# Attention scores of two heads side by side in the row halves of TensorE, and the shared expert's two projections in one matmul group

## The chip, the cores and the metric

The kernel runs on 1 core of one Trainium2 chip. The metric is the time of one execution on the device in microseconds (us). A core has TensorE (PE, with its weight loads shown apart as PEld), VectorE (DVE), ScalarE (ACT), GpSimd (POOL) and the DMA queues, most of them issued from SyncE (SP). Each engine works through its own list of instructions in order, and they wait for each other by semaphores.

## What is computed

One transformer layer on x of 8 sequences of 256 tokens with 128 channels, all in float32. Attention has 16 heads of 8 channels; the feed-forward part has a shared expert and 16 routed ones (top 2), each of width 64.

```
xn = layernorm(x)
qkv = xn @ Wqkv + bqkv ; q, k = rope(q), rope(k)
probs = softmax(q @ k.T / sqrt(8))            # 8 x 16 heads, 256 x 256 each
attn = (probs @ v) @ Wout + bout
router = sigmoid(xn @ gate_w + gate_b) ; top 2 values, divided by their sum
mlp(x, wg, wu, wd) = (silu(x @ wg) * (x @ wu)) @ wd
ffn = xn + mlp(xn, shared) + sum over the top 2 of value * mlp(xn, expert)
out = x + attn + ffn
```

## The kernel before

**Tiles.** Two sequences make a group of 512 tokens, 4 groups in all. The feed-forward part is cut into chunks of 128 hidden rows, 9 to a group and 36 in all, numbered n: chunk 0 of a group (n = 0, 9, 18, 27) is the shared expert and fills only 64 rows, and the other eight hold two experts each. The attention is cut into 32 steps q of four heads. Two steps make a half (h = 0 to 15), that is eight heads of one sequence.

**Blocks.** One list of 40 blocks, blk = -6 to 33, sets the order on every engine. Block blk holds chunk n = blk + 6, the row maxima of the scores of step q = blk + 4, the exponentials of the scores of step blk, and the product with the values of step blk - 1. Each block has four places, i = 0 to 3, one head at each. The tables `LATE_A` and `EARLY_B` say in which block the rarer work stands (transposes of x, projections of q, k and v, the router, the transposes and projection of the attention's output).

**Scores.** q and k are split into bfloat16 parts, laid out so that six products of parts stand as 48 rows (`KROWS`). A pair of heads shares a slot: head r of the pair has rows 48r to 48r + 47 of `q_hat`, and `k_hat` holds each head's rows with zeros in the other head's rows, so that a matmul over 96 rows gives one head. `max_scores` (L508) makes two 256-column matmuls for a head into one of the two PSUM banks `S1a`, `S1b`, whose maxima DVE takes (`TENSOR_REDUCE`, L1000). For each half POOL splits the negated maxima into three bfloat16 parts (`negate_maxima`, L1072 to L1076, result `md`), PE transposes them (L497, `maxima_to_rows`) into an S1 bank, DVE copies them to `mT` (L872), and a DMA puts them as 6 more rows below the 96 of `q_hat` (L336). `exp_scores` (L529) then computes scores minus maximum over 102 rows into `S2a` or `S2b`, and ACT takes the exponential (L734) into `probs`. `attend` (L548) multiplies four heads' probabilities with the values, four matmuls of 32 columns side by side. PE takes one bank at a time: scores for a bank wait only until that bank's former contents are read.

**Feed-forward.** `up(n, "hg")` makes the gate product of chunk n in three matmuls (float32 as high and low parts, L386 to L388) into bank `FA`, and `up(n, "hu")` the up product into `FB`. ACT takes the tanh of FA (L746) and from n = 6 on copies FA to `gate` (L750). DVE multiplies tanh + 1 with FB (`gu`, L988; for n < 6 two operations, L1009 and L985). POOL weights gate and product (L1112, L1114, L1101), and `down` (L581) of chunk n - 2 adds to bank `Y`.

**Order on PE in a block.** i = 0: exponential's scores, maximum's scores, gate product, in every second block the transposes of the maxima of a half; i = 1: `attend`, scores; i = 2: `EARLY_B` work, scores; i = 3: `down`, `LATE_A` work, scores, up product. "Scores" are two matmuls into an S2 bank and two into an S1 bank. POOL and DVE take their parts of the block in the same order; POOL does `negate_maxima` first, then the weighting, then residuals and the splits of the next group's q and k.

## Time and profile before

| | us |
|---|---|
| median of 3 runs | 243.12 |
| lowest, highest | 242.80, 243.15 |
| the profiled execution | 242.69 |
| its span, first to last instruction | 240.0 |
| PE, DVE, POOL, ACT busy | 216.0, 168.7, 161.2, 137.1 |

A row of the timeline gives the start of the first instruction in it, the time until the last one's end, engine, line, operation, output <- inputs, shapes and count, and in brackets the idle time before it with the instruction that ended it. On PE the pair such as 96*128 is the rows and columns of the array that the matmul uses. Matmuls are pipelined: a row's duration contains the way through the array, so what a matmul costs its follower is the distance of the starts. A row can merge several instructions.

### The profile page before, as it was taken

Reading aid. Unit: us, or ns where it says so; the run is one execution under the profiler, and the core shown is the slowest. Engines: PE = TensorE matmul, PEld = TensorE weight load, DVE = VectorE, ACT = ScalarE, POOL = GpSimd, SP = SyncE. Lnnn points to the kernel's source line nnn. Section 1 sums busy time; section 2 is a strip of 40 time slices with the busy share of each in tenths; the row PEclk is TensorE's granted clock in tenths of the full one; section 3 lists DMA queues with packets and bytes.
Section 4 is the critical chain, followed back from the end, with each engine's and each line's share of the span. In section 5 each row is a group of like instructions: output and inputs, shape, how many; then the busy total and the mean of one; then the engine's idle time right before and its main releaser. Section 6 shows DMA issues by size and latency. Waiting matters only on the chain.

```text
span 240.0 us, 4717 instructions
## 1 busy us (share of the span) xinstructions
PE 216.0 (90%) x1576; PEld 134.1 (56%) x1576; DVE 168.7 (70%) x374; ACT 137.1 (57%) x257; POOL 161.2 (67%) x236
## 2 busy tenths in 40 slices
PE   0485698898989999989999999999999999999993
PEld 0354454464655666666756656666756656675552
DVE  5997869999585766998656768976666666655221
ACT  2455111155568665656566665667575866667662
POOL 9186763789847259888848295999893855637802
PEclk9997789999999999999999999999999999999999
DMA  6925354620527240502662414116516450211101
GB/s 231 358 66 152 104 163 131 189 92 2 182 71 219 80 145 5 153 0 75 204 202 60 159 46 126 30 54 175 150 31 190 142 155 17 76 50 43 47 0 44
DMA packets 35952, 26.51 MB, mean 110 GB/s; under 512 B 4236, under 2 KB 30156, under 8 KB 35916
## 3 DMA queue, kind: packets, MB, share of 16 engines
q1 hardware_dynamic: 35292, 25.33, 34.9%
q10 hardware_dynamic: 636, 0.88, 1.0%
q8 instruction: 12, 0.20, 0.3%
q14 instruction: 12, 0.10, 0.1%
HBM read 18.53 MB, written 7.47 MB: 108 GB/s over the span
## 4 chain that ended last, share of the span: by engine, by line
PE 74%; DVE 11%; DMA 5%; SPq 4%; issue 2%; ACT 2%; POOL 1%; DVEq 0%; ACTq 0%; POOLq 0%
PE PV L548 12%; PE Y L581 12%; PE S2b L529 7%; PE S2a L529 6%; PE S1a L508 5%; PE S1b L508 5%; PE FB L386 3%; PE FB L387 3%; PE FB L388 3%; PE FA L387 3%; PE FA L386 3%; PE FA L388 3%; DMA x_sb<-in_x 2%; DVE mx L1000 2%; PE FA L441 2%
## 5 line engine op out<-in xcount | busy, mean ns | idle before, releaser
L1000 DVE TENSOR_REDUCE mx<-S1a 128x2 f32<-128x512 f32 x65 | 44.6, 686 | 17.3 <-PE S1a L508 17.3
L1000 DVE TENSOR_REDUCE mx<-S1b 128x2 f32<-128x512 f32 x63 | 43.2, 685 | 19.2 <-PE S1b L508 19.0
L734 ACT ACTIVATE probs<-S2b 128x512 f32<-128x512 f32 x62 | 37.1, 598 | 29.5 <-PE S2b L529 29.5
L734 ACT ACTIVATE probs<-S2a 128x512 f32<-128x512 f32 x62 | 37.1, 599 | 17.2 <-PE S2a L529 14.6
L1114 POOL TENSOR_TENSOR gu<-gu,gate 128x512 f32<-128x512 f32 (+1 forms) x30 | 38.2, 1274 | 9.1 <-DVE gu L988 7.6
L581 PE MATMUL Y<-gu,wd_sb 128*128 128x512 f32 (+1 forms) x72 | 37.3, 599 | 0.3 <-POOL gu L1101 0.3
L746 ACT ACTIVATE th<-FA 128x512 f32<-128x512 f32 (+1 forms) x36 | 21.5, 597 | 25.3 <-PE FA L388 25.1
L548 PE MATMUL PV<-probs,vx 128*32 128x256 f32 x512 | 35.1, 384 | 0.2 <-ACT probs L734 0.2
L1112 POOL TENSOR_TENSOR gate<-gate,wbc 128x512 f32<-128x512 f32 x27 | 34.5, 1279 | 0.7 <-DMA wbc<-route_w 0.6
L508 PE MATMUL S1a<-k_hat,q_hat 96*128 96x256 bf16 x130 | 25.2, 275 | 1.5 <-DVE mx L1000 1.5
L508 PE MATMUL S1b<-k_hat,q_hat 96*128 96x256 bf16 x126 | 24.3, 274 | 1.6 <-DVE mx L1000 1.4
L529 PE MATMUL S2a<-q_hat,k_hat 102*128 102x256 bf16 x124 | 24.1, 276 | 0.0
L529 PE MATMUL S2b<-q_hat,k_hat 102*128 102x256 bf16 x124 | 24.1, 275 | 0.0
L988 DVE SCALAR_TENSOR_TENSOR gu<-th,FB 128x512 f32<-128x512 f32 (+1 forms) x30 | 20.4, 679 | 1.8 <-PE FB L388 1.6
L548 PEld LDWEIGHTS PV<-probs,vx 128*32 128x32 f32 x512 | 16.0, 109 | 9.7 <-ACT probs L734 4.7
L529 PEld LDWEIGHTS S2b<-q_hat,k_hat 102*128 102x128 bf16 x124 | 9.2, 97 | 20.8 <-issue 17.2
L386 PE MATMUL FB<-xT_hi,wu_hi 128*128 128x512 f32 (+1 forms) x36 | 17.7, 492 | 3.0 <-ACT sig L685 2.7
L386 PE MATMUL FA<-xT_hi,wg_hi 128*128 128x512 f32 (+1 forms) x36 | 17.5, 486 | 0.6 <-ACT xT L667 0.4
L750 ACT ACTIVATE gate<-FA 128x512 f32<-128x512 f32 (+1 forms) x30 | 17.7, 590 | 0.0
L1072 POOL TENSOR_SCALAR md<-mx 128x16 bf16<-128x16 f32 x16 | 3.3, 205 | 21.3 <-DVE mx L1000 21.3
L508 PEld LDWEIGHTS S1b<-k_hat,q_hat 96*128 96x128 bf16 x126 | 11.7, 99 | 7.1 <-DVE mx L1000 4.9
L529 PEld LDWEIGHTS S2a<-q_hat,k_hat 102*128 102x128 bf16 x124 | 9.1, 98 | 11.2 <-issue 6.3
(163 smaller groups left out, 408.4 us busy)
## 6 DMA issues: line engine op xcount, KB each, us to landing
wbc<-route_w SPq DMA_DIRECT2D x64, 128.0 KB, 3.0
q_hat<-q_parts SPq DMA_DIRECT2D x32, 96.0 KB, 2.6
k_hat<-k_parts SPq DMA_DIRECT2D x32, 96.0 KB, 2.6
k_parts<-parts SPq DMA_DIRECT2D x8, 192.0 KB, 2.1
q_parts<-parts SPq DMA_DIRECT2D x8, 192.0 KB, 2.2
x_sb<-in_x SPq DMA_DIRECT2D x4, 256.0 KB, 3.9
q_parts<-parts SPq DMA_DIRECT2D x8, 128.0 KB, 2.1
k_parts<-parts SPq DMA_DIRECT2D x8, 128.0 KB, 2.1
```

Of the source, the lines that this page charges most:

```text
L386: nc.tensor.matmul(bank, w_hi, m_hi, start=start, stop=False)
L508: last = nc.tensor.matmul(bank[:, t * T:(t + 1) * T], q_hat[0:MROW, slot, pair, t * P:(t + 1) * P], k_hat[0:MROW, slot, pair, r, :], start ...
L529: last = nc.tensor.matmul(exp_bank(head)[:, s * T:(s + 1) * T], k_hat[0:KALL, slot, pair, r, s * P:(s + 1) * P], q_hat[0:KALL, slot, pair, ...
L548: last = nc.tensor.matmul(PV[32 * j:32 * j + 32, hg * T:(hg + 1) * T], vx[:, (b // GB) % 2, SB * (b % GB) + s, r, NQ * hg + j, :], probs[: ...
L581: nc.tensor.matmul(Y[:], wd_sb[0:rows, c, :], gu[0:rows, n % GU_SLOTS, :], start=c == 0, stop=c == NCH - 1).then_inc(down_done, 1)
L734: nc.scalar.activation(probs[:, head % (2 * NQ), :], exp_bank(head)[:], ACT.Exp, scale=SCALE).then_inc(exp_done, 1)
L746: nc.scalar.activation(th[0:rows, n % 2, :], FA[0:rows, :], ACT.Tanh, scale=0.5).then_inc(th_ready, 1)
L750: nc.scalar.activation(gate[0:rows, n % 2, :], FA[0:rows, :], ACT.Copy, scale=0.5 if n % NCH == 0 else 1.0).then_inc(fa_read, 1)
L988: nc.vector.scalar_tensor_tensor(gu[0:rows, m % GU_SLOTS, :], th[0:rows, m % 2, :], 1.0, FB[0:rows, :], ALU.add, ALU.mult).then_inc(fb_rea ...
L1000: nc.vector.tensor_reduce(mx[:, (q // QB) % 2, (q // 2) % 2, :, q % 2, i], S1[use % 2][:].rearrange("p (t s) -> p t s", t=SB), axis=AX.X, ...
L1112: after(nc.gpsimd.tensor_tensor(gates, gates, wbc[:, g % 2, c - 1, :], ALU.mult))
L1114: nc.gpsimd.tensor_tensor(product, product, gates, ALU.mult).then_inc(gu_weighted, 1)
```

## The change

The scores move into row halves of the array. Head r of a pair now has its 48 rows at partition 64r of `q_hat` and `k_hat`, and its three maxima rows behind them, so that a matmul runs over 48 (51 with the maxima) rows in one half of the array. `max_pair` and `exp_pair` take two heads at a time, in opposite halves and into both banks in turn. `k_hat` loses its zeros (two memsets and the wait for them go), and the ones and the maxima come by two DMAs each where one stood. Which head of a pair is at which half alternates with the step (`score_row_half`).

The order in a block changes: the gate product stands first; scores come in two lots, at i = 0 and i = 2; transposes of the maxima, `down` and `LATE_A` work move to i = 2 ahead of the second lot, so the transposes of a half come half a block earlier. On ACT the tanh comes at i = 0 and the copy of the gate after the second exponential.

For the shared expert the gate and up weights stand side by side, one group of three matmuls fills FA (gate in rows 0 to 63, up in rows 64 to 127), and no second group is made; DVE multiplies straight from FA at i = 1, and POOL weights that product as any other. For n = 0 one DVE operation less is made.

```diff
-    last = nc.tensor.matmul(bank[:, t * T:(t + 1) * T], q_hat[0:MROW, slot, pair, t * P:(t + 1) * P],
-                            k_hat[0:MROW, slot, pair, r, :], start=True, stop=True)
-last.then_inc(s1_ready, 1)
...
+banks = [take_s(("max", q * NQ + i)) for i in (first, first + 1)]
+for t in range(SB):
+    for i, bank in zip((first, first + 1), banks):
+        pair, rows = NQ * hg + i, HROWS * score_row_half(q, i)
+        last = nc.tensor.matmul(bank[:, t * T:(t + 1) * T],
+                                q_hat[rows:rows + KROWS, slot, pair, t * P:(t + 1) * P],
+                                k_hat[rows:rows + KROWS, slot, pair, :], start=True, stop=True)
+        if t == SB - 1:
+            last.then_inc(s1_ready, 1)
...
 if head < NQ * FOUR_BANKS + 2:
     if head >= 2:
-        pe.wait_ge(exp_done, head - 1)
+        pe.wait_ge(exp_done, head)
...
+for s in range(SB):
+    for i in (first, first + 1):
+        pair, rows = NQ * hg + i, HROWS * score_row_half(q, i)
+        last = nc.tensor.matmul(exp_bank(q * NQ + i)[:, s * T:(s + 1) * T],
+                                k_hat[rows:rows + KALL, slot, pair, s * P:(s + 1) * P],
+                                q_hat[rows:rows + KALL, slot, pair, :], start=True, stop=True)
...
 for i in range(NQ):
+    if i == 0 and n < NCHUNKS:
+        up(n, "hg")
     if i == 1 and 0 <= blk - 1 < NBLK:
         attend(blk - 1)
     if i == 2:
         for kind, g in early_b(blk):
             fill_b(kind, g)
-    if i == 3 and 0 <= n - 2 < NCHUNKS:
-        down(n - 2)
-    if i == 3:
+        if 0 <= n - 2 < NCHUNKS:
+            down(n - 2)
+        if negated_half(blk) is not None:
+            maxima_to_rows(negated_half(blk))
         for kind, g in late_a(blk):
             fill_a(kind, g)
-    if 0 <= blk < FOUR_BANKS:
-        exp_scores(blk, i)
-    if 0 <= q < NBLK:
-        max_scores(q, i)
-    if i == 0 and n < NCHUNKS:
-        up(n, "hg")
+    if i % 2 == 0 and 0 <= blk < FOUR_BANKS:
+        exp_pair(blk, i)
+    if i % 2 == 0 and 0 <= q < NBLK:
+        max_pair(q, i)
...
-    if i == 0 and transposed_half(blk) is not None:
-        maxima_to_rows(transposed_half(blk))
-    if i == 3 and n < NCHUNKS:
+    if i == 3 and n < NCHUNKS and n % NCH:
         up(n, "hu")
...
+    if m % NCH == 0:
+        dve.wait_ge(th_ready, m + 1)
+        dve.wait_ge(shared_gate, m // NCH + 1)
+        nc.vector.scalar_tensor_tensor(product, tanh, 1.0, FA[I:2 * I, :], ALU.add, ALU.mult).then_inc(fa_read, 1)
+        return
```

How this moves PE's instructions is seen in block 18, from `attend` (PV) to its third lot of scores. Before:

```order
L548 MATMUL PV<-probs,vx 32x256 x8
L529 MATMUL S2b<-q_hat,k_hat 128x256 x2
L508 MATMUL S1b<-k_hat,q_hat 128x256 x2
L482 MATMUL FB<-ident_sb,attn 128x128 x2
L529 MATMUL S2a<-q_hat,k_hat 128x256 x2
L508 MATMUL S1a<-k_hat,q_hat 128x256 x2
L581 MATMUL Y<-gu,wd_sb 128x512
L529 MATMUL S2b<-q_hat,k_hat 128x256 x2
L508 MATMUL S1b<-k_hat,q_hat 128x256 x2
```

After (L575 is `attend`, L611 `down`, L517 the transposes of the maxima, L555 the exponential's scores, L530 the maximum's):

```order
L575 MATMUL PV<-probs,vx 32x256 x8
L502 MATMUL FB<-ident_sb,attn 128x128 x2
L611 MATMUL Y<-gu,wd_sb 128x512
L517 MATMUL S1a<-identb_sb,md 24x128 x2
L555 MATMUL S2a<-q_hat,k_hat 128x256
L555 MATMUL S2b<-q_hat,k_hat 128x256
L555 MATMUL S2a<-q_hat,k_hat 128x256
L555 MATMUL S2b<-q_hat,k_hat 128x256
L530 MATMUL S1b<-k_hat,q_hat 128x256
L530 MATMUL S1a<-k_hat,q_hat 128x256
L530 MATMUL S1b<-k_hat,q_hat 128x256
L530 MATMUL S1a<-k_hat,q_hat 128x256
```

Four lots of two and two score matmuls, each lot for one head, have become lots of eight for two heads, banks in turn. `down` and the transposes of the maxima stand before the second lot.

The boundary from there to the next block's `attend`, before:

```order
L529 MATMUL S2a<-q_hat,k_hat 128x256 x2
L508 MATMUL S1a<-k_hat,q_hat 128x256 x2
L386 MATMUL FA<-xT_hi,wg_hi 128x512
L387 MATMUL FA<-xT_hi,wg_lo 128x512
L388 MATMUL FA<-xT_lo,wg_hi 128x512
L497 MATMUL S1b<-identb_sb,md 24x128 x2
L548 MATMUL PV<-probs,vx 32x256 x8
```

After, from the gate product on:

```order
L406 MATMUL FA<-xT_hi,wg_hi 128x512
L407 MATMUL FA<-xT_hi,wg_lo 128x512
L408 MATMUL FA<-xT_lo,wg_hi 128x512
L555 MATMUL S2a<-q_hat,k_hat 128x256
L555 MATMUL S2b<-q_hat,k_hat 128x256
L555 MATMUL S2a<-q_hat,k_hat 128x256
L555 MATMUL S2b<-q_hat,k_hat 128x256
L530 MATMUL S1b<-k_hat,q_hat 128x256
L530 MATMUL S1a<-k_hat,q_hat 128x256
L530 MATMUL S1b<-k_hat,q_hat 128x256
L530 MATMUL S1a<-k_hat,q_hat 128x256
L575 MATMUL PV<-probs,vx 32x256 x8
```

The gate product stands ahead of all scores of the block, and the transposes of the maxima are gone from the place before `attend`.

On ACT, a block with the attention's transpose read at i = 1, before:

```order
L746 ACTIVATE th<-FA 128x512
L750 ACTIVATE gate<-FA 128x512
L734 ACTIVATE probs<-S2b 128x512
L697 ACTIVATE attnT<-FB,bias_sb 128x256
L734 ACTIVATE probs<-S2a 128x512
L734 ACTIVATE probs<-S2b 128x512
L734 ACTIVATE probs<-S2a 128x512
```

After (L772 tanh, L763 exponential, L782 copy of the gate, L726 the transpose's read):

```order
L772 ACTIVATE th<-FA 128x512
L763 ACTIVATE probs<-S2a 128x512
L763 ACTIVATE probs<-S2b 128x512
L782 ACTIVATE gate<-FA 128x512
L726 ACTIVATE attnT<-FB,bias_sb 128x256
L763 ACTIVATE probs<-S2a 128x512
L763 ACTIVATE probs<-S2b 128x512
```

The copy of the gate (L750, now L782) has moved from right behind the tanh to behind the first two exponentials of the block.

## Rows read from the trace of the kernel before

**Rows 1.** The page: busy time of each engine and TensorE's granted clock in 40 slices.

```profile
PE 216.0 (90%) x1576; PEld 134.1 (56%) x1576; DVE 168.7 (70%) x374; ACT 137.1 (57%) x257; POOL 161.2 (67%) x236
...
PEclk9997789999999999999999999999999999999999
```

**Rows 2.** Busy time by stretch: us, PE, PEld, DVE, ACT, POOL, clock, DMA share, GB/s.

```profile
28.00:62.00 34.00, 30.35 (x165) 17.50 (x165) 29.50 (x64) 11.19 (x22) 23.91 (x40) 0.95 0.39 117
62.00:222.00 160.00, 158.02 (x1239) 99.46 (x1237) 112.38 (x218) 104.59 (x196) 111.74 (x170) 1.00 0.35 103
222.00:240.00 18.00, 13.99 (x122) 7.89 (x121) 4.13 (x12) 9.56 (x19) 6.42 (x6) 1.00 0.08 30
...
98.50:105.30 6.80, 6.80 (x56) 4.51 (x56) 6.60 (x21) 4.52 (x9) 6.30 (x11) 1.00 0.27 70
```

**Rows 3.** Waits of PE from 62 to 222 us: total, times, longest.

```profile
PE S1a L508 <- DVE mx L1000: 0.8, 1, 0.8
PE S1b L508 <- DVE mx L1000: 0.6, 1, 0.6
PE FA L386 <- ACT xT L667: 0.4, 1, 0.4
PE PV L548 <- ACT probs L734: 0.2, 1, 0.2
```

**Rows 4.** Timeline of PE over one block, from 178.6 us.

```profile
178.60 0.39 PE L388 MATMUL FA<-xT_lo,wg_hi 128*64 128x512 f32 x1
178.92 0.23 PE L497 MATMUL S1a<-identb_sb,md 128*24 128x128 bf16 x1
...
179.04 1.03 PE L548 MATMUL PV<-probs,vx 128*32 128x256 f32 x13
180.00 0.39 PE L529 MATMUL S2b<-q_hat,k_hat 102*128 102x256 bf16 x2
180.23 0.38 PE L508 MATMUL S1b<-k_hat,q_hat 96*128 96x256 bf16 x2
180.45 0.38 PE L529 MATMUL S2a<-q_hat,k_hat 102*128 102x256 bf16 x2
180.67 0.38 PE L508 MATMUL S1a<-k_hat,q_hat 96*128 96x256 bf16 x2
180.89 1.02 PE L581 MATMUL Y<-gu,wd_sb 128*128 128x512 f32 x2
181.75 0.60 PE L433 MATMUL FA<-ident_sb,pv_sb 128*128 128x128 f32 x4
182.19 0.38 PE L529 MATMUL S2b<-q_hat,k_hat 102*128 102x256 bf16 x2
182.41 0.38 PE L508 MATMUL S1b<-k_hat,q_hat 96*128 96x256 bf16 x2
...
183.33 0.39 PE L529 MATMUL S2a<-q_hat,k_hat 102*128 102x256 bf16 x2
```

**Rows 5.** Timeline of PE around the shared expert's `down`, 64 rows of the array.

```profile
82.87 0.38 PE L508 MATMUL S1a<-k_hat,q_hat 96*128 96x256 bf16 x2
83.18 1.12 PE L581 MATMUL Y<-gu,wd_sb 64*128 64x512 f32 x2
84.24 0.66 PE L433 MATMUL FA<-ident_sb,pv_sb 128*128 128x128 f32 x4
```

**Rows 6.** Timeline at the first transposes of maxima: PE's `down`, POOL's last part, transposes, copy.

```profile
43.04 1.02 PE L581 MATMUL Y<-gu,wd_sb 128*128 128x512 f32 x2
...
45.42 0.20 POOL L1076 TENSOR_SCALAR md<-mrest 128x16 bf16<-128x16 f32 x1
...
45.95 0.28 PE L497 MATMUL S1b<-identb_sb,md 128*24 128x128 bf16 x2
...
46.34 0.27 DVE L872 COPY mT<-S1b 24x256 bf16<-24x256 bf16 x1
```

**Rows 7.** Timeline at the first router weights, 26.5 to 27.7 us.

```profile
26.56 0.38 DVE L865 TENSOR_TENSOR wtok<-wsel 128x64 f32<-128x64 f32 x1
26.87 0.67 DVE L985 TENSOR_TENSOR gu<-FB,th 64x512 f32<-64x512 f32 x1
...
27.69 0.27 PE L470 MATMUL FB<-ident_sb,wtok 128*64 128x128 f32 x1 [1.55 <-DVE gu L985]
```

**Rows 8.** The page's groups: busy time, mean ns, idle before.

```profile
L1000 DVE TENSOR_REDUCE mx<-S1a 128x2 f32<-128x512 f32 x65 | 44.6, 686 | 17.3 <-PE S1a L508 17.3
...
L734 ACT ACTIVATE probs<-S2b 128x512 f32<-128x512 f32 x62 | 37.1, 598 | 29.5 <-PE S2b L529 29.5
```

224 lines of the change are left out of this document (117 added, 107 removed).

## The prediction

> **What bounds the kernel now.** I read the page first: PE is busy for 216.0 of 240.0 us, DVE for 168.7, and TensorE's clock is at nine tenths or more from the seventh of the 40 slices on [rows 1]. The table by stretch splits the run: from 62 to 222 us PE is busy for 158.02 of 160 us and no other engine for more than 112.38; from 28 to 62 us DVE is the fullest, with 29.50 of 34; the last 18 us are a tail with little in it [rows 2]. In the long middle PE's waits add up to 2.0 us [rows 3]. So there every bit of stream taken from PE counts, as long as its partners keep up. Then comes PE's timeline over one block [rows 4], read by the distances of starts, since the durations (0.38 us) contain the way through the array. Two score matmuls take 180.00 to 180.23, and eight take 180.00 to 180.89: 0.111 us each. `down` takes 180.89 to 181.75, 0.86. A three-matmul group takes 0.70 (182.41 + 0.22 to 183.33). `attend` with the transposes of the maxima takes 178.92 to 180.00. The block is a full stream: 16 score matmuls are 1.78 us of a plain block, with two such groups (1.40), `down` (0.86) and `attend` (1.07) 5.1.
>
> **Row halves.** Each lot of eight becomes four rounds of two matmuls side by side, if the halves run together. A round should cost what one matmul costs, 0.111 us. The trace has no matmuls in two row halves at once; it has four in column strips, where 13 of the 16 of `attend`, of 256 columns, end 1.03 us after the first start [rows 4], where one after another they would take more than 13 x 0.111 = 1.44. The bounds for a round are 0.111 (both together) and 0.222 (one after another). I take 0.111, because the column strips are the nearest case. That is 0.89 us less for each of the 27 blocks (1 to 27) with both kinds of scores: **-24.0 us**. At 0.222 it is 0.
>
> The Trainium skill, "TensorE: Matmul & The Clock Gate", section "Measured speedup vs the span model", gives 3.07 times for four row tiles, not 4. By that a round would cost 1.3 times a matmul, and 7 us of the 24 would be gone; rows of this case can't decide it, since none has two row tiles at work.
>
> **What the halves cost.** The shared expert's `down` already works in 64 rows, and shows the price of changing the division of the array [rows 5]. The scores before it start at 82.87, and two take 0.22, so it could start at 83.09; it starts at 83.18: 0.09 for the change. From there to the next instruction is 1.06 us against 0.86 for the same work in 128 rows [rows 4], 0.20 more: 0.09 for the change back, and 0.11 because the first weights of a float32 operand no longer load under the matmul before. The step into the 24-column transposes costs the same 0.09 (178.60 + 0.23 to 178.92) [rows 4].
>
> A block before has two changes (into `attend` and out). After, it has five: gate product to scores, scores to `attend`, `attend` to `down`, `down` to scores, scores to up product. Three more at 0.09 are 0.27. The first weights lie bare twice more, before `down` and before the up product: 0.21. Together 0.48 a block, 27 blocks: **+13.0 us**. The low bound is 0.27 a block, 7.3 us, if the weights still load in time. The scores' own weights are bfloat16, and behind `attend` today two matmuls start 0.23 apart as elsewhere [rows 4], so I count nothing for them.
>
> **Transposes of the maxima** (every second block, 14 times in this stretch). They lie between `down` and scores, where they cost one change more: 0.09 x 14 = 1.3. And they hold an S1 bank. From their start to the end of DVE's copy is 45.95 to 46.61 [rows 6], 0.66 us; `max_pair` takes both banks before it starts, and PE has only the transposes, a change and four exponential's scores to issue, about 0.43. The 0.23 left is a wait in the 7 of these blocks where no `LATE_A` work stands between and maxima follow: 1.6. Together **+2.9 us**.
>
> **Shared expert.** Three of the four (n = 9, 18, 27) are in this stretch. Each saves a group of three, 0.70, and its `down` follows `attend` and precedes scores in the same halves, so that the 0.29 of rows 5 and one change of 0.09 go: 1.08 x 3 = **-3.2 us**. DVE, ACT and POOL have as many operations for it as before (for n = 0 DVE has one of 0.67 less [rows 7]).
>
> **The partners.** A lot of exponential's scores now waits until both former banks are read. From lot to lot across the block's end: ACT can start 0.39 after the first start, and two exponentials of 0.598 [rows 8] end at 1.6; PE's own way is two half lots (0.44), 0.20 of change and weights, 0.70 + 0.70 for up and gate product, 0.09, together 2.13. Two maxima of 0.686 [rows 8] end 1.98 after the exponential's lot began (0.22 + 0.39 + 1.37), and are wanted at 2.35. The other distance, with `attend` and `down` in it, is 2.6. So the pairs are covered in a plain block, by 0.4 to 0.5 us; without that cover each would show in full. ACT has six operations of about 0.6 in a plain block and DVE 3.4 us (four maxima and a product), and the tanh that now comes before the first exponential falls into ACT's gap. Where it isn't covered is the block from 98.5: DVE is busy for 6.60 of 6.80 and POOL for 6.30 [rows 2]; it and its twin eight blocks later gain nothing and lose what they were counted: **+0.8 us**. POOL runs late in a few blocks, and the transposes of the maxima now ask for its result half a block earlier: **+1.0 us**, an estimate between 0 and 3.
>
> **The first 62 us.** DVE sets the pace there, and it lives on two banks in turn. With pairs it stands for about 0.4 us after its second read, unless other work fills that. Ten lots are in question; I count three (bounds 0 and 10 x 0.4): +1.2. The first transposes of maxima are wanted right after `down`, at 43.04 + 0.86 = 43.9; POOL's last part is ready at 45.62 [rows 6]. PE stands for up to 1.7 us there with `max_pair` queued behind, DVE behind that; I take 1.5. Against it, the router's transpose at 27.69 waited for a DVE read of FB (26.87 to 27.54) that is gone, while its input was ready at 26.94 [rows 7]: -0.6 on a chain that goes on by DMAs; and one DVE operation of 0.67 less. In sum **+1.5 us**.
>
> **At nothing.** Both memsets of `k_hat` ran while x was on its way. SP issues two more DMAs for the ones, before it has to wait for q and k. The maxima go by two DMAs of half the size; they start half a block earlier and are wanted in the second block after; if that lead were gone, each would cost its issue of some 0.4 us. The tail has changes that eat the halved scores.
>
> **Sum.** -24.0 + 13.0 + 2.9 - 3.2 + 0.8 + 1.0 + 1.5 = -8.0 us. The profiled execution took 242.69, of which 240.0 is the span and the rest stays, so 234.7; the median of the runs is 0.4 above it. I predict **235.1 us**, likeliest case 229 to 239.5.
>
> **Rivals.**
> (a) Slower: *the row halves run one after another*. The changes and bare weights stay, the 24.0 go: 259. The gain is nil where a round of two costs 0.147 us (27 x 8 rounds x (0.222 - 0.147) = 16). Against it: the column strips. Chance 0.07.
> (b) *Halves overlap in part*, since one weight path feeds both: a round between 0.13 and 0.17 gives 239 to 248, centre 243. Chance 0.13 (0.04 still faster, 0.02 the same, 0.07 slower).
> (c) *The pairs wait*: PE ahead, and the reads of both banks end last. At 0.2 us a block the gain shrinks by 5 to 240 or 241. For it: DVE has only 0.37 (2.35 - 1.98) of cover, and every operation beyond the plain ones eats from it. Chance 0.15 (0.02 of it the same). The Trainium skill, "TensorEngine Tiling (Array Packing)", section "PSUM Bottleneck", says that tiling speeds the engine up but not the reading of its results; by that, reading is next in line, which is this case.
> (d) *The first third loses more*: all ten lots stand (4.0), and POOL's lateness recurs at each transposes of maxima (0.5 x 14): 244 to 247. Chance 0.07.
> (e) Weights load in time after a change, and the waits are small: 13.0 - 7.3 = 5.7 less and a little more, 227 to 229. Chance 0.06.
>
> **Numbers.** The likeliest case has 0.52. Faster by over 0.2%: 0.52 + 0.06 + 0.13 + 0.04 = 0.75; within 0.2%, which is about what a measurement here can tell apart: 0.04; slower: 0.07 + 0.07 + 0.07 = 0.21. The range of 228 to 247 leaves out (a), the end of (b) and half of (e).
>
> **What would show it.** In the timeline of PE after, two score matmuls of opposite halves start within some hundredths of a us, and a lot of eight takes 0.44 to 0.50 from its first start to the end of its stream, with 0.09 before it and 0.20 behind it. Plain blocks last 4.7 instead of 5.1. PE's share stays above 90% in the middle and its waits there for DVE's maxima and copy are 2 to 4 us. The first `attend` of the middle comes 1 to 2 us later than before. The forecast is wrong if lots take 0.9 (a), or if PE's waits in the middle are above 6 us (c).

## The result, and the profile after

The changed kernel took 248.74 us in the median of four executions (246.70 to 250.83), the one before 243.13 beside it on the same chip: ratio 1.0195, 95% interval 1.0146 to 1.0243. A second set, run later, gave 247.36 in the median of six (245.85 to 250.34) and 1.0127 (1.0077 to 1.0176). The change makes the kernel 1 to 2% slower; 235.1 was predicted, with a range of 228 to 247. So the sign was wrong, and both medians lie outside the range. Here and below, a ratio leaves out the executions that took over 1.5% longer than the shortest of their kernel, while a median holds them all, so the two need not rank two kernels alike.

The page of the changed kernel, against [rows 1]: PE has less to do, 207.4 us instead of 216.0, and still the span is 244.3 instead of 240.0. The third line is the granted clock of TensorE in 40 slices.

```profile
span 244.3 us, 4751 instructions
...
PE 207.4 (85%) x1564; PEld 110.3 (45%) x1564; DVE 164.1 (67%) x372; ACT 131.1 (54%) x258; POOL 159.5 (65%) x235
...
PEclk9999799689999999999997999999999999999998
```

The table by stretch of the changed kernel (columns as in [rows 2]):

```profile
28.00:62.00 34.00, 26.00 (x141) 13.54 (x145) 26.01 (x58) 7.99 (x17) 20.80 (x34) 0.90 0.40 107
62.00:222.00 160.00, 151.08 (x1233) 79.47 (x1225) 112.22 (x221) 97.90 (x194) 111.83 (x169) 0.99 0.36 105
```

In the first stretch both PE and DVE work less per us than before: 26.0 for 30.35, and 26.0 for 29.50. Before, PE and DVE were nearly full there; now none is. In the long middle PE stands for 8.9 us where it stood for 2.0. Some of its waits there, the longest sums first (us in total, times, longest):

```profile
PE S2a L555 <- ACT probs L763: 1.5, 2, 0.8
PE FA L431 <- DVE gu L972: 1.1, 1, 1.1
PE S1b L530 <- DVE mT L912: 1.0, 5, 0.2
PE FB L490 <- DVE gu L977: 1.0, 1, 1.0
```

Over half of all that are listed there, 4.6 of 8.4 us, stand at the banks FA and FB and not at the scores' banks.

A simple ruler for where time goes is the start of the gate product of each chunk, since both kernels have 36. Chunk 8's began at 61.36 before and at 64.87 after (67.25 in the second set's profile), chunk 35's at 221.29 and at 225.38 (226.81). So 3.5 to 5.9 us are lost by chunk 8, and the 27 blocks between take 159.93 us before and 160.51 (159.56) after. The prediction had +1.5 for the start and -9.5 for those blocks. Behind them, to the end of the span, it is 18.7 us and 19.0 (18.9).

The 27 blocks by themselves, before and after (columns as in [rows 2]):

```profile
61.35:221.29 159.94, 157.96 (x1241) 99.47 (x1238) 112.36 (x218) 104.74 (x195) 111.68 (x170) 1.00 0.35 105
```

```profile
64.87:225.38 160.51, 151.59 (x1233) 79.72 (x1232) 111.82 (x220) 98.60 (x196) 112.12 (x172) 0.99 0.34 101
```

PE's busy time fell by 6.4 us and its idle time rose by 6.9. The sum had 12.9 us less work for PE (-24.0 + 13.0 + 1.3 - 3.2) and 3.4 us more waiting (1.6 + 0.8 + 1.0). A busy row holds the way through the array as well, so a short stop shows as less idle time than it costs.

**The halves themselves work.** PE's timeline of the changed kernel around a gate product and the lot behind it:

```profile
183.42 0.40 PE L408 MATMUL FA<-xT_lo,wg_hi 128*128 128x512 f32 x1
183.75 0.28 PE L555 MATMUL S2a<-q_hat,k_hat 51*128 51x256 bf16 x1
183.75 0.28 PE L555 MATMUL S2b<-q_hat,k_hat 51*128 51x256 bf16 x1
183.87 0.27 PE L555 MATMUL S2a<-q_hat,k_hat 51*128 51x256 bf16 x1
...
183.98 0.27 PE L530 MATMUL S1a<-k_hat,q_hat 48*128 48x256 bf16 x1
...
184.09 0.27 PE L530 MATMUL S1a<-k_hat,q_hat 48*128 48x256 bf16 x1
184.09 0.27 PE L530 MATMUL S1b<-k_hat,q_hat 48*128 48x256 bf16 x1
184.29 0.42 PE L575 MATMUL PV<-probs,vx 128*32 128x256 f32 x4
```

Two matmuls of opposite halves start together, and a round takes 0.11 us (183.87 to 183.98), what one matmul took in [rows 4]. Behind the last round 0.20 pass to the next instruction: 0.11 of work and 0.09 for the change of the array's division. Both terms stand as predicted. I measure a block from the start of one PV group to the next, and number it by the PV group (1 to 32) that ends it. Blocks with nothing but the plain work fell by 0.44 to 0.50 us (blocks 20, 26 and 28: -0.49, -0.44, -0.49); the sum had 0.89 - 0.48 = 0.41.

**The blocks with transposes of the maxima don't gain.** Blocks 19, 21, 23, 25 and 27 take 0.12 to 0.18 us *more* than before. PE's timeline of one of them, and the copy on DVE:

```profile
191.28 1.02 PE L611 MATMUL Y<-gu,wd_sb 128*128 128x512 f32 x2
192.24 0.28 PE L517 MATMUL S1a<-identb_sb,md 128*24 128x128 bf16 x2
192.45 0.28 PE L555 MATMUL S2a<-q_hat,k_hat 51*128 51x256 bf16 x1
...
192.58 0.27 PE L555 MATMUL S2b<-q_hat,k_hat 51*128 51x256 bf16 x1
193.05 0.27 PE L530 MATMUL S1b<-k_hat,q_hat 48*128 48x256 bf16 x1 [0.20 <-DVE mT L912]
...
192.63 0.28 DVE L912 COPY mT<-S1a 24x256 bf16<-24x256 bf16 x1 [1.17 <-PE S1a L517]
```

The transposes hold PE's stream for 0.21 us (192.24 to 192.45); the maxima's scores begin 0.60 behind the exponential's (192.45 to 193.05) instead of 0.23, since `max_pair` needs both banks of the ring and DVE reads one of them until 192.91; and one more change of division lies before them. That is 0.21 + 0.37 + 0.09 = 0.67 us. Of the 0.37, 0.23 is the wait until the copy's end, and 0.14 passes from there to the first score. In the kernel before they ran beside the PV group, whose first matmuls stand between the two transposes:

```profile
178.92 0.23 PE L497 MATMUL S1a<-identb_sb,md 128*24 128x128 bf16 x1
178.94 0.42 PE L548 MATMUL PV<-probs,vx 128*32 128x256 f32 x3
```

A stretch from gate product to the scores behind PV was 0.08 us longer with them (1.95) than without (1.87).

**The first transposes of the maxima** are the longest stop behind the first 24 us. PE and POOL of the changed kernel:

```profile
41.65 1.02 PE L611 MATMUL Y<-gu,wd_sb 128*128 128x512 f32 x2
44.93 0.39 PE L517 MATMUL S1a<-identb_sb,md 128*24 128x128 bf16 x2 [2.26 <-POOL md L1118]
...
44.67 0.20 POOL L1118 TENSOR_SCALAR md<-mrest 128x16 bf16<-128x16 f32 x1
```

PE stands for 2.26 us behind POOL, where before it met the finished parts [rows 6]. The gate product of chunk 4 starts 1.2 us earlier than before, that of chunk 5 2.7 us later. No other wait of PE for POOL is in this profile.

**The merged shared expert.** ACT, DVE and PE of the changed kernel around the gate product of chunk 27:

```profile
183.85 0.59 ACT L772 ACTIVATE th<-FA 64x512 f32<-64x512 f32 x1 [1.11 <-PE FA L408]
...
185.30 0.59 ACT L780 ACTIVATE gate<-FA 64x512 f32<-64x512 f32 x1
...
186.02 0.69 DVE L972 SCALAR_TENSOR_TENSOR gu<-th,FA 64x512 f32<-64x512 f32 x1 [0.34 <-ACT gate L780]
...
186.86 0.63 PE L453 MATMUL FA<-ident_sb,pv_sb 128*128 128x128 f32 x4 [0.44 <-DVE gu L972]
...
188.40 0.50 PE L406 MATMUL FA<-xT_hi,wg_hi 128*128 128x512 f32 x1 [0.37 <-DVE attn L949]
```

The merged product lies in FA, and FA is free only when ACT has read it twice and DVE once, one after another, at 186.71. The transposes of `LATE_A` wait for that, the next gate product waits for their reader, and in this block the saved matmuls come to nothing: it takes 0.08 us more than before.

### The profile page after: what moved, and what is told of

Read it like the earlier page. It is cut to its first block, busy times and chain, and to the rows that moved or that the text cites. A ratio compares the mean times of both kernels' runs of the same rounds, so it can differ in the third digit from the quotient of the medians.

```text
span 244.3 us, 4751 instructions
## 1 busy us (share of the span) xinstructions
PE 207.4 (85%) x1564; PEld 110.3 (45%) x1564; DVE 164.1 (67%) x372; ACT 131.1 (54%) x258; POOL 159.5 (65%) x235
## 4 chain that ended last, share of the span: by engine, by line
PE 62%; DVE 16%; issue 8%; POOL 6%; ACT 4%; DMA 2%; SPq 0%; DVEq 0%; POOLq 0%; ACTq 0%
PE PV L575 11%; PE Y L611 11%; PE FB L406 5%; PE S2a L555 5%; DVE mx L1045 4%; PE FA L406 3%; PE S1a L530 3%; PE FB L408 3%; PE S1b L530 3%; PE FB L407 3%; PE FA L408 3%; PE FA L407 3%; ACT probs L763 2%; DMA x_sb<-in_x 2%; PE FA L461 2%
## 5 line engine op out<-in xcount | busy, mean ns | idle before, releaser
L763 ACT ACTIVATE probs<-S2a 128x512 f32<-128x512 f32 x62 | 36.9, 595 | 34.9 <-PE S2b L555 34.1
L1152 POOL TENSOR_TENSOR gu<-gu,gate 128x512 f32<-128x512 f32 (+1 forms) x31 | 39.4, 1273 | 14.1 <-DVE gu L977 10.0
L772 ACT ACTIVATE th<-FA 128x512 f32<-128x512 f32 (+1 forms) x36 | 21.5, 596 | 42.6 <-PE FA L408 37.9
L611 PE MATMUL Y<-gu,wd_sb 128*128 128x512 f32 (+1 forms) x72 | 40.0, 638 | 0.0
L763 ACT ACTIVATE probs<-S2b 128x512 f32<-128x512 f32 x62 | 37.2, 600 | 0.0
L575 PE MATMUL PV<-probs,vx 128*32 128x256 f32 x512 | 34.9, 391 | 0.0
L530 PE MATMUL S1a<-k_hat,q_hat 48*128 48x256 bf16 x128 | 24.8, 274 | 6.0 <-DVE mx L1045 3.7
L530 PE MATMUL S1b<-k_hat,q_hat 48*128 48x256 bf16 x128 | 24.9, 274 | 1.6 <-DVE mT L912 1.5
L555 PE MATMUL S2a<-q_hat,k_hat 51*128 51x256 bf16 x124 | 24.1, 274 | 1.8 <-ACT probs L763 1.8
L555 PE MATMUL S2b<-q_hat,k_hat 51*128 51x256 bf16 x124 | 24.1, 275 | 0.0
L406 PE MATMUL FA<-xT_hi,wg_hi 128*128 128x512 f32 x36 | 15.2, 422 | 6.1 <-DVE gu L972 4.1
L977 DVE SCALAR_TENSOR_TENSOR gu<-th,FB 128x512 f32<-128x512 f32 x27 | 18.3, 678 | 1.4 <-PE FB L408 1.4
L575 PEld LDWEIGHTS PV<-probs,vx 128*32 128x32 f32 x512 | 13.5, 110 | 12.3 <-issue 6.7
L782 ACT ACTIVATE gate<-FA 128x512 f32<-128x512 f32 x27 | 16.7, 618 | 0.0
L406 PE MATMUL FB<-xT_hi,wu_hi 128*128 128x512 f32 x32 | 16.2, 506 | 0.5 <-ACT wT L720 0.5
L555 PEld LDWEIGHTS S2a<-q_hat,k_hat 51*128 51x128 bf16 x124 | 6.9, 94 | 20.1 <-issue 17.4
L530 PEld LDWEIGHTS S1a<-k_hat,q_hat 48*128 48x128 bf16 x128 | 10.4, 95 | 11.3 <-DVE mx L1045 5.1
L407 PE MATMUL FA<-xT_hi,wg_lo 128*128 128x512 f32 x36 | 14.7, 409 | 0.0
```

What stands on the lines that cost most here:

```text
L406: nc.tensor.matmul(bank, w_hi, m_hi, start=start, stop=False)
L407: nc.tensor.matmul(bank, w_lo, m_hi, start=False, stop=False)
L530: last = nc.tensor.matmul(bank[:, t * T:(t + 1) * T], q_hat[rows:rows + KROWS, slot, pair, t * P:(t + 1) * P], k_hat[rows:rows + KROWS, sl ...
L555: last = nc.tensor.matmul(exp_bank(q * NQ + i)[:, s * T:(s + 1) * T], k_hat[rows:rows + KALL, slot, pair, s * P:(s + 1) * P], q_hat[rows:r ...
L575: last = nc.tensor.matmul(PV[32 * j:32 * j + 32, hg * T:(hg + 1) * T], vx[:, (b // GB) % 2, SB * (b % GB) + s, score_row_half(q, j), NQ * ...
L611: nc.tensor.matmul(Y[:], wd_sb[rows, c, :], gu[rows, n % GU_SLOTS, :], start=c == 0, stop=c == NCH - 1).then_inc(down_done, 1)
```

## The experiments

Medians with the ratio to the kernel before, which was run beside each (its medians: 242.85 to 243.64). Names join edits: `unmerged` means that the shared expert has its own up group again, which holds for m_ahead_pv_2, m_ahead_pv_2_obo, m_behind_pv_obo and best too; `obo` means that the maxima's scores of the first eight score blocks go one head after the other. All are made from the changed kernel, except before_m_moved. Gate products 8 and 35 are starts in the profiled execution of each, less before's.

| run | median us | ratio (95%) | gate 8 | gate 35 |
|---|---|---|---|---|
| the change | 248.74 | 1.0195 (1.0146 to 1.0243) | +3.5 | +4.1 |
| after_again | 247.36 | 1.0127 (1.0077 to 1.0176) | +5.9 | +5.5 |
| one_half | 266.31 (one) | | +9.5 | +23.3 |
| m_late | 247.53 | 1.0142 (1.0066 to 1.0219) | +3.9 | +5.2 |
| unmerged | 245.83 | 1.0110 (1.0052 to 1.0168) | +6.6 | +3.8 |
| m_late_unmerged | 246.08 | 1.0054 (1.0008 to 1.0101) | +4.1 | +3.9 |
| filled | 245.92 | 1.0105 (1.0029 to 1.0182) | +4.3 | +3.9 |
| one_by_one_start | 245.00 | 1.0077 (1.0040 to 1.0114) | +5.9 | +8.0 |
| m_in_fa | 245.44 | 1.0091 (1.0053 to 1.0129) | +5.9 | +3.9 |
| m_in_fa_unmerged | 244.79 | 1.0060 (1.0019 to 1.0101) | +6.5 | +2.4 |
| before_m_moved | 249.35 | 1.0151 (1.0102 to 1.0201) | +5.9 | +8.2 |
| m_ahead_pv_unmerged | 251.36 | 1.0350 (1.0278 to 1.0422) | +2.8 | +8.2 |
| m_ahead_pv_unmerged_obo | 250.99 | 1.0302 (1.0227 to 1.0377) | +4.5 | +10.0 |
| m_ahead_pv_2 | 243.80 | 0.9979 (0.9937 to 1.0020) | +4.2 | +1.2 |
| m_ahead_pv_2_obo | 244.83 | 0.9953 (0.9906 to 1.0000) | +2.0 | +0.9 |
| merged_m_ahead_pv_obo | 243.22 | 0.9960 (0.9923 to 0.9997) | +2.8 | +3.2 |
| m_behind_pv_obo | 245.18 | 1.0038 (1.0004 to 1.0072) | +1.5 | +3.8 |
| merged_m_behind_pv_obo | 247.54 | 1.0132 (1.0090 to 1.0173) | +4.6 | +7.4 |
| best | 240.84 | 0.9895 (0.9838 to 0.9951) | +2.1 | -4.1 |

> The changed kernel itself once more, so that the others of this set are compared with it on the same chip in many executions. Its median of four executions was 248.7 us with a spread of 4 us; if the spread is that of the half-clock stretches of the first 65 us, the median of more executions lies between 246 and 249 us, and the executions again spread over 3 to 4 us.

The second set of the change came out as expected, and shows that its executions differ by 4.5 us; a difference of 1 us between two rows tells nothing by itself.

### Do the halves run side by side, and does PE's stream set the pace?

one_half puts both heads of a pair into the rows from 0 up. It leaves out the scores of the heads in rows 64 up and computes those of the others twice.

```
-                        pair, rows = NQ * hg + i, HROWS * score_row_half(q, i)
+                        pair, rows = NQ * hg + i, 0
```

> The changed kernel with both heads of a pair read from rows 0 and up, so that no two score matmuls stand in opposite halves; the heads of the upper half get the scores of the lower half's heads, so the output isn't the reference's. All other work is the same. If two halves really work side by side and PE sets the pace: a round of two takes 0.22 instead of 0.11 us, 216 rounds and 14 to 16 of the tail later the run is 15 to 24 us longer, 263 to 272. If waits, not PE's stream, set the pace now: 250 to 256.

It took 266.31 us. PE's timeline of one_half, one lot:

```profile
203.66 0.28 PE L555 MATMUL S2a<-q_hat,k_hat 51*128 51x256 bf16 x1
203.78 0.27 PE L555 MATMUL S2b<-q_hat,k_hat 51*128 51x256 bf16 x1
203.89 0.27 PE L555 MATMUL S2a<-q_hat,k_hat 51*128 51x256 bf16 x1
204.00 0.27 PE L555 MATMUL S2b<-q_hat,k_hat 51*128 51x256 bf16 x1
204.21 0.27 PE L530 MATMUL S1a<-k_hat,q_hat 48*128 48x256 bf16 x1
```

The same instructions start 0.11 apart, and the kernel, in its one execution, is 17.6 to 19 us longer than the changed one. The 27 blocks for which the 24.0 was counted take 173.70 us, 13.2 to 14.1 more than in the changed kernel's two profiles:

```profile
70.86:244.56 173.70, 171.32 (x1233) 98.46 (x1232) 110.30 (x220) 99.65 (x195) 112.57 (x171) 1.00 0.32 93
```

PE stands for 2.4 us of them where it stood for 8.9 in the changed kernel. So in time the halves are worth 13 to 14 of the 24.0 there; about 6.5 us of the difference is idle time that the longer stream fills, and the rest I have not found.

### The transposes of the maxima: three places

m_late gives them back their old place in time, one block later, between the gate product and the first pair, in the scores' ring as before; m_late_unmerged has the shared expert's own up group with it.

```
-                    if i == 1 and negated_half(blk) is not None:
+                    if i == 0 and transposed_half(blk) is not None:
...
                     if i == 0 and n < NCHUNKS:
                         up(n, "hg")
+                    if i == 0 and transposed_half(blk) is not None:
+                        maxima_to_rows(transposed_half(blk))
```

> The changed kernel with one thing put back: the transposes of the maxima stand in the next block, between the gate product and the first lot of scores, as half a block later as before the change. Theory A (PE's early stop for POOL's maxima parts, 2.3 us at the first half, the half-rate clock after it and the wait for DVE's copy are what ate the gain): the gate product of n = 5 comes about 3 us earlier than in the changed kernel, no stretch at half clock between 44 and 51 us, time 241 to 243. Rival B (the pairs' waits and bare weights take the gain all along, wherever the transposes stand): 247 to 249.

> Both put back: transposes of the maxima half a block later, shared expert in two groups; row halves, pairs and the gate product first stay. If A and C both hold and add up: 237 to 240, faster than before the change. If only A: 241 to 243. If neither: 248 to 252.

At first m_late did what was expected: the stop for POOL was gone, and chunk 5's gate product was only 0.6 us later than before instead of 2.7. But the time stayed, and by chunk 8 it was 3.9 us late all the same, with TensorE's clock at half from 57.2 to 64.0 us. Behind the transposes the first pair of scores wants both banks, and DVE's copy stands behind what DVE has left over from the block before: m_late_unmerged waits for mT 5.6 us (7 times) ahead of S1a and 3.2 us (8 times) ahead of S1b. The expectation of 237 to 240 was missed by 6 us. It had taken the loss for one of the place alone.

m_in_fa takes the transposes out of the scores' ring: they have a turn of FA at the end of the block, and the pairs don't wait for them.

```
-                bank = take_s(("M", h)).bitcast(bf16)
+                take_a(("M", h))
+                bank = FA.bitcast(bf16)
```

> The changed kernel with one difference: the transposes of the maxima no longer take a bank of the scores' ring of two (S1a, S1b) but a turn of the gate bank FA, between the second pair of scores and the up product. Theory T (the transposes cost much because a pair needs both banks of the ring, so that it waits for DVE's copy of the transposed maxima, which was hidden behind the one other bank before): the waits of S1a and S1b for mT vanish, the blocks with transposes (+0.1 us against before in the changed kernel) come to about -0.4 like the plain ones, 14 x 0.5 = 7 us, less what was already idle elsewhere: 241 to 244 us. Rival (the transposes cost their own time and two array changes wherever they stand, or DVE is simply late and the wait moves to the next gate product, which now waits for the copy): 247 to 249 us.

> The same, and the shared expert's up product a matmul group of its own again, as before the change. Theory T plus the 2.9 us that the run without the merge showed: 238 to 241 us, below the kernel before. Rival (the two losses hide behind each other, or the start until 60 us, where about 4 us are lost, is what is left): 243 to 246 us. The middle of the kernel, from the gate product of chunk 8 to that of chunk 30, should then shrink against before by 22 blocks x 0.4 = 9 us by T, by less than 4 us by the rival.

The blocks 19 to 27 that have them went from +0.12 to +0.18 to -0.02 to -0.14 us against before: 0.20 to 0.27 less each, where 0.5 was expected, and 245.44 us is 1.4 above the range of theory T. Its ratio and the change's overlap; from chunk 8 to 35 its profile has 157.93 us for 160.51 and 159.56. The wait for the copy is gone, the 0.21 of the transposes' own stream isn't. From chunk 8 to 35 m_in_fa_unmerged is 4.1 us below before, and yet 1.006 in the ratio, since it is 6.5 us late at chunk 8.

In the next runs the transposes go where PE has cover for their stream as before, right ahead of `attend`, a block later than the change has them, but in a turn of FB.

```
+                    if i == 1 and transposed_half(blk) is not None:
+                        maxima_to_rows(transposed_half(blk))
                     if i == 1 and 0 <= blk - 1 < NBLK:
                         attend(blk - 1)
```

> The changed kernel, the shared expert's up product a group of its own again, and the transposes of the maxima taken out of the scores' ring: in a turn of FB, right ahead of the PV group of the next block, where before had them next to that group too. In before's trace a transposes' place there costs TensorE 0.08 us of stream (1.951 us from the gate product to the scores behind PV with them, 1.875 without); in the changed kernel it costs 0.09 (down product to next start 0.52 for 0.43) + 0.215 + 0.37 (wait for DVE's copy ahead of the pair) = 0.67 us. Theory T: the blocks with transposes fall from +0.1 to about -0.4 us against before, 14 x 0.5 = 7 us less than the unmerged kernel's 245.8, of which what DVE and the second queue take back is lost: 238 to 242 us, gate product 28 at -4 to -5 us of its distance to gate product 8. Rival (the start's loss and the waits on ACT and DVE take up whatever TensorE's stream gives): 244 to 246 us.

> m_ahead_pv_unmerged with SyncE's load of the transposed maxima issued where before had it, ahead of the scratch copies of its block, instead of one block later. In m_ahead_pv_unmerged the load of block 10 stood behind a copy that waited 12.8 us for POOL, and the scores behind PV waited 5.1 us for it; up to the gate product of chunk 15 it was only 1.06 us behind the kernel before. If that misplaced load is what cost, all from chunk 16 on comes 8 to 10 us earlier: 239 to 242 us, and gate product 35 within 1.5 us of before's 221.3. Rival: the queue is held by the next load instead, because the transposes come a quarter of a block later than before, 245 us or more.

m_ahead_pv_unmerged was a mistake of mine that shows a queue: I had also moved SyncE's load of the maxima one block on. PE's and SP's waits of that kernel, from 105 to 130 us:

```profile
PE S2a L558 <- DMA q_hat<-mT: 5.1, 1, 5.1
...
SPq L337 <- POOL parts L295: 12.8, 1, 12.8
```

The load stood behind a scratch copy that waited 12.8 us for POOL. With the load where before had it (m_ahead_pv_2) the kernel took 243.80, 0.9979 (0.9937 to 1.0020): level with before, 1.5% under the change run beside it, and 2 us above what was expected. Its twin with obo in the name has 0.12 us from the start of the transposes to that of PV (below), where before had 0.02.

### Is it the pairs, or the place?

before_m_moved answers that from the other side. It is the kernel before, heads one at a time over the whole array, with only the transposes put where the change has them, behind `down` in the block in which POOL finishes.

```
                     if i == 3 and 0 <= n - 2 < NCHUNKS:
                         down(n - 2)
+                    if i == 3 and negated_half(blk) is not None:
+                        maxima_to_rows(negated_half(blk))
```

> The kernel before with one difference: the transposes of the maxima in the block in which POOL makes them ready, behind the down product (where the change puts them), heads still one at a time and over the whole array. Theory T (they cost through the pair that needs both banks of the ring): only their own stream shows, 0.08 to 0.2 us each, and the wait for POOL at the first one, 244 to 247 us. Rival (the place by itself is what costs, 0.6 us each, and the late first transposes take 3 us): 249 to 254 us, the first gate products behind it 3 us late.

It took 249.35 us, 1.0151 of before (1.0102 to 1.0201): about as slow as the whole change. In its profile, of an execution of 250.86 us, chunk 8 is at 67.25, 5.9 us late, and the 27 blocks to chunk 35 take 2.3 us more, 0.16 for each of the 14. Of before_m_moved, two lines of PE's timeline, the largest wait of PE from 28 to 62 us, and that stretch in the table:

```profile
43.18 1.02 PE L581 MATMUL Y<-gu,wd_sb 128*128 128x512 f32 x2
45.80 0.39 PE L497 MATMUL S1b<-identb_sb,md 128*24 128x128 bf16 x2 [1.59 <-POOL md L1076]
...
PE S1b L508 <- DVE mx L1002: 3.2, 4, 1.9
...
28.00:62.00 34.00, 27.67 (x124) 15.32 (x125) 27.14 (x58) 7.50 (x16) 19.91 (x33) 0.86 0.34 105
```

So I expected rightly for the middle and wrongly for the start: a loss there needs no pairs. PE stands for POOL's result, and DVE has less to reduce (27.14 busy of 34, for 29.50 in [rows 2]). How large that loss is, this profile overstates. Its clock was at half from 45.4 to 48.9 and from 59.1 to 62.5 us, which before's was not, and its two shortest executions took 246.61 and 247.85 us, 3.3 and 4.6 above before's median of 243.28. If the middle takes its 2.3 us in them too, 1 to 2.3 us are left for the start, about the stop of 1.59 itself; the rest of the 5.9 is what this one execution added.

In the blocks 19 to 27 with transposes this kernel takes 0.29 us more than before, in those between 0.06 less: neighbours differ by 0.35. In the changed kernel they differ by 0.6 (+0.12 to +0.18, against -0.44 to -0.49). So of the 0.6 the place alone explains 0.35, and the pair's claim on both banks 0.25, which is what m_in_fa gave back.

### The start: the clock, and the pair's claim on two banks

In the changed kernel the clock fell to half in the stretches around the stops of PE: 23.7 to 27.1 us and 44.2 to 51.0. That is 10.2 us before chunk 8, where the second set's profile has 17.0, and before's 6.8. filled puts matmuls that serve nothing where PE stood.

```
+                    if n == 1:
+                        filler(16)
                     take_a(("hg", n))
...
+                if h == 0:
+                    filler_bank[0] = take_s(("M", h))
+                    filler(8)
                 pe.wait_ge(md_ready, h + 1)
```

> The changed kernel with matmuls that compute nothing of use put where TensorE stood still at the start: 16 of 512 columns ahead of the gate product of chunk 1 (the 4.1 us until 23.5), 8 ahead of the first transposes of maxima (the 2.3 us until 44.9). Theory C (the start loses 4 us because TensorE stands still and its clock is then granted at half for 3.5 us from 23.7 and for 6.8 us from 44.2): no slice below 0.9 in 44 to 51, 2 to 5 us less, 244 to 246.5 us. Rival (the start's pace is set by DVE and POOL, and the half clock only falls into waits that would be there anyway): 247.5 to 250 us, the gate product of chunk 8 at 64 to 66 us as in the changed kernel.

The table by stretch, first filled, then the changed kernel:

```profile
42.00:52.00 10.00, 8.39 (x45) 4.79 (x45) 7.21 (x14) 0.97 (x3) 7.20 (x15) 1.00 0.50 127
52.00:64.00 12.00, 9.69 (x62) 4.96 (x58) 9.56 (x30) 5.82 (x12) 9.14 (x15) 0.86 0.25 75
```

```profile
42.00:52.00 10.00, 7.28 (x27) 3.57 (x26) 5.71 (x12) 0.72 (x2) 6.62 (x13) 0.66 0.54 143
52.00:64.00 12.00, 9.69 (x74) 4.62 (x72) 9.88 (x31) 5.92 (x13) 8.13 (x14) 1.00 0.20 60
```

The half clock of 44 to 51 us is gone (1.00 for 0.66) and another came at 58.6 to 62.0. Chunk 8's gate product starts at 65.70, not earlier than in the changed kernel. The median of 245.92 is where theory C wanted it, but the start is as its rival said, and the intervals of the two ratios overlap widely (1.0105 and 1.0127). So filling the stops moved the half clock and gained nothing that can be told from noise. 6.8 us at half were left before chunk 8, as many as in the kernel before, and it still began 4.3 us late. So more time at half clock isn't what makes this start late; what a start at full clock would take, no run here shows.

one_by_one_start and the runs with obo in their name take the second bank of a pair only behind the first head's matmuls, in the first eight score blocks.

```
-                banks = [take_s(("max", q * NQ + i)) for i in (first, first + 1)]
-                for t in range(SB):
-                    for i, bank in zip((first, first + 1), banks):
+                if q < ONE_BY_ONE:
+                    order = [(i, t) for i in (first, first + 1) for t in range(SB)]
```

> The changed kernel with that alone: the maxima's scores of the first eight score blocks head by head, each waiting for its own bank. Theory P: VectorE busy 26 us or more of 30 to 62 us, gate product 8 at 61.5 to 63.5 us instead of 64.9, 245 to 247.5 us. Rival: gate product 8 at 64.5 to 66 us, 248 to 250 us.

> The same, and in the first eight score blocks the maxima's scores head by head: the first head's two matmuls wait for their own bank alone, and the second bank is taken only behind them. Theory P (with the pair both banks of the ring must be free before either is written, so VectorE and TensorE take turns where VectorE sets the pace, 30 to 62 us: VectorE busy 24.3 of 32 us in the changed kernel, 28.0 before): the start regains 2 to 3 us of the 4 lost, 236 to 239.5 us. Rival (the start loses through TensorE's wait for POOL's md and the half clock): no less than 1 us from the kernel without it.

> The same with the maxima's scores head by head in the first eight score blocks. Theory P (the pair's wait for both banks costs 2 to 3 us while VectorE sets the pace): 237 to 240.5 us, 1 to 2.5 below m_ahead_pv_2. Rival (no effect; the two one-by-one runs so far differ from their partners by -0.4 and -3.7 us in the median): within 0.8 us of m_ahead_pv_2.

No pair of runs settles it. one_by_one_start has 1.0077 where the change has 1.0195 and 1.0127, but its profiled execution, the longest of its eleven, was 5.9 us late at chunk 8. m_ahead_pv_2_obo has 0.9953 against 0.9979, with overlapping intervals, and from chunk 4 to 8 both profiles take the same (22.67 and 22.76 us; before 21.18, the change 25.92). m_ahead_pv_unmerged_obo, with the misplaced load, is level with its partner too. What the claim on both banks costs at the start stays open: nothing by the last two pairs, 1.2 to 2.9 us by the ratios of the first.

### The shared expert's merge

unmerged gives the up product a group of its own in FB again.

```
-        if n < NCHUNKS and n % NCH:
+        if n < NCHUNKS:
             b["hu", n] = len(b)
...
-            return (0, 2 * I) if c == 0 else (2 * I + (c - 1) * P, 2 * I + c * P)
+            return (0, I) if c == 0 else (2 * I + (c - 1) * P, 2 * I + c * P)
```

> The changed kernel with one thing put back: the shared expert has its own group of matmuls for the up product into FB. Theory C (the merged group costs more than the 0.70 it saves, because FA is held until DVE's product, behind ACT's copy at i = 1, and what needs FA next waits): 1 us less for each of three blocks and up to 1 us at the start, 244.5 to 246. Rival D (the merge saves 1.08 us in each of three blocks, as the sum of the prediction had it): 251 to 252.

> The same with the shared expert's gate and up products merged, as the change has them. By the 2.9 us between the changed kernel and the unmerged one: 2 to 3.5 us above m_ahead_pv_2_obo, 240 to 243 us. Rival (the merge cost only in the company of the pairs' waits): within 1 us of m_ahead_pv_2_obo.

unmerged took 245.83 us, as expected. Three pairs differ by the merge alone: the change and unmerged (1.0195 and 1.0127, against 1.0110), merged_m_ahead_pv_obo and m_ahead_pv_2_obo (0.9960 and 0.9953), merged_m_behind_pv_obo and m_behind_pv_obo (1.0132 and 1.0038). In none does the merge gain in the ratio; that it loses is clear of noise in the third pair alone. The medians of the second pair lie the other way, 243.22 with the merge and 244.83 without. In the profiles the merged kernel takes longer from chunk 8 to 35 in all three: 160.51 and 159.56 against 157.10, 160.39 against 158.76, 162.69 against 162.22. The three blocks with the merge, blocks 4, 13 and 22, are 1.3, 1.5 and 0.6 us longer in the change than in unmerged. The 1.5 holds a half-clock stretch; in the second set's profile, which has none there, the three are 0.9, 0.0 and 0.6.

### The last waits

m_ahead_pv_2_obo still stood for 5.2 us between 62 and 222 us, 4 times, ahead of the transposes: PE's timeline at the longest but one.

```profile
158.16 0.27 PE L541 MATMUL S1b<-k_hat,q_hat 48*128 48x256 bf16 x1
160.41 0.27 PE L521 MATMUL FB<-identb_sb,md 128*24 128x128 bf16 x2 [1.97 <-DVE gu L981]
160.53 1.07 PE L586 MATMUL PV<-probs,vx 128*32 128x256 f32 x16
```

In this block and its twin eight blocks earlier DVE's product, which frees FB, stands behind the routing's steps. m_behind_pv_obo puts all transposes behind the PV group; best moves only those of loads 5 and 9, into a turn of FA at the end of the block before.

```
+EARLY_HALVES = (5, 9)
...
+                early = h in EARLY_HALVES
+                (take_a if early else take_b)(("M", h))
+                bank = (FA if early else FB).bitcast(bf16)
```

> m_ahead_pv_2_obo with the transposes of the maxima behind the PV group instead of ahead of it, DVE's copy of them behind its second reduction. In m_ahead_pv_2_obo five of them waited for FB, which DVE's product had not left, 5.4 us in all, longest 2.1, and the gate products of chunks 16 and 24 lost 1.5 and 3.7 us against before. Theory F (those waits cost as they read): PV covers 1 us of each, 2 to 3.5 us less than m_ahead_pv_2_obo, fast executions at 239 to 241.5 us. Rival (the load of the maxima, now 1 us later, or a change of array division more per transposes, takes it back): the same time within 1 us.

> The same with the shared expert's products merged as in the change. By the pair of runs before (243.2 against 244.8, ratios 0.996 and 0.995) the merge is worth nothing there: within 1 us of m_behind_pv_obo. If the saved products (3 x 1.08 us) come through once nothing waits at FB: 1 to 3 us below it.

> m_ahead_pv_2_obo with two of its fourteen transposes of maxima elsewhere: those of the loads 5 and 9, which waited 2.05 and 1.94 us at FB for DVE's product (it stands behind the routing's steps in those blocks), go into a turn of FA at the end of the block before, where m_in_fa_unmerged had them and lost nothing at the gate products of chunks 16 and 24 (-0.7 and -0.02 us, where m_ahead_pv_2_obo lost 1.5 and 3.7). Theory F: 3 to 5 us less, executions without a late half-clock stretch at 237.5 to 240.5 us, below the kernel before by 1 to 2%. Rival (the wait goes to the next product or to the scores, as it did when the transposes went behind PV): 242 us or more.

Behind PV nothing was won: the next uses of FB now waited for DVE's copy (2.2, 1.7, 1.3 and 0.9 us in four rows of the waits) and the scores 2.3 us for the load. best took 240.84 us (237.98 to 241.89), 0.9895 of before (0.9838 to 0.9951), faster than both kernels, as theory F had it. Of its six executions five are shorter than the shortest of before's eleven, 241.79. Its table by stretch and its largest waits of PE in the middle:

```profile
28.00:62.00 34.00, 29.58 (x148) 15.33 (x148) 28.18 (x61) 9.28 (x19) 22.17 (x37) 0.90 0.39 102
62.00:222.00 160.00, 153.82 (x1289) 85.34 (x1288) 112.75 (x224) 102.49 (x203) 117.54 (x176) 1.00 0.37 108
...
PE FB L532 <- DVE gu L996: 1.1, 2, 0.9
PE S2a L577 <- ACT probs L789: 1.1, 2, 0.8
```

From chunk 8 to chunk 35 it takes 153.69 us, 6.2 less than before. That is the prediction's middle with its two losses mostly gone (-24.0 + 13.0 = -11.0 by the sum), less 4.8 us; where these stay I have not followed block by block. PE's idle time of 6.2 us in that stretch, where before had 2.0, is most of it.

## Why the prediction was wrong

- **Row halves, -24.0.** Right as a price: a round is 0.11. As time in the 27 blocks, one_half puts it at 13.2 to 14.1 us.
- **What the halves cost, +13.0.** Right. Changes are 0.09 each and the bare weights as counted; plain blocks fell by 0.44 to 0.50 for 0.41.
- **Transposes of the maxima, +2.9, and POOL late, +1.0.** The first of two steps that failed in the middle. I counted a change in each and a wait of 0.23 in seven blocks. The rows show 0.67 us in one with the wait: I had left out the transposes' own 0.21, which before lay beside the PV group for 0.08, and the wait delays the scores by 0.37. At 0.6 more in the seven blocks that wait for the copy and 0.35 in the seven others, the place's share, it is an estimated 6.7 us. The wait for POOL did not recur; it is one stop, in the start.
- **Shared expert, -3.2.** The second step, and by the profiles no smaller. The stream of PE does get shorter by the matmuls, but the sum looked only at that. FA now holds two results for three reads, and the transposes and the gate product behind it queue for the bank. Three pairs of runs show a gain in none; against unmerged the changed kernel's 27 blocks are 2.5 and 3.4 us longer instead of 3.2 shorter.
- **The first 62 us, +1.5.** Wrong: 3.5 and 5.9 in two profiles. The stop for POOL was seen and sized fairly (1.5 to 1.7; it was 2.26). before_m_moved shows that the place alone costs the start something, 1 to 2.3 us by its shorter executions. It isn't the whole: m_late has no such stop and was 3.9 us late at chunk 8. More time at half clock (10.2 and 17.0 us by then, for 6.8) goes with the longer start, 5.9 for 3.5, but filled had no more than before and was 4.3 us late. How the loss divides between the stop, the clock and DVE standing between the pairs is open. The rows had a sign of it: PE with 30.35 of 34 us was busier there than DVE with 29.50 [rows 2], not DVE the fullest, as I read them.
- **The partners, +0.8.** About right for plain blocks; the pairs of scores there wait for nobody. The dense block from 98.5, of which no gain was expected, takes 1.3 us more than before (2.4 in the second profile), and the one behind it 1.2 (1.3) less.
- **The rivals.** (a), (b) and (e) fell with the timeline. (c) had part of the middle, the pair's claim on both banks, but not in the plain blocks where I looked: only with a third user in the ring of two. The sign that was named for it, waits of PE above 6 us in the middle, did come, with 8.9, and more than half of them stand at FA and FB, of which (c) says nothing. (d) came nearest, with its 244 to 247 for 247.4 and 248.7: the first third loses more. That is nearness of the number: POOL's lateness, its 7 us, did not recur, and its cause for the start, ten lots with DVE standing, is not shown. It had 0.07, and should have had far more, since the sum's small terms were each read from one side.

The gain from the halves is real, then. In the middle it went into two things that the change did beside it and did not need; at the start the loss is only in part explained.

## What to carry to other kernels

When heads are taken in pairs from a ring of two banks, every other user of that ring is better out of it, since with the pair nothing is left to hide it: here 0.25 us in each block that waits for the copy. A step that asks for another engine's result should keep its distance to it: moving it up by half a block, with nothing else changed, made the kernel before 1.5% slower, about as much as the whole change. And matmuls merged into one bank save stream only if the bank isn't held longer than what is queued for it can bear.
